# A Toeplitz chunk's eight lag matrices stored side by side, loaded as 4 KB rows and read by TensorE with a step of eight

## What is computed

```python
ew = jnp.exp(wc); ek = jnp.exp(k)             # k = v = the context
Af, Bf = _wkv_scan(ek, v, ew)                 # forward: A_t = sum_{i<t} e^{(t-1-i)w + k_i} v_i, B_t without v
Ab, Bb = _wkv_scan(ek[:, ::-1], v[:, ::-1], ew)
cur = jnp.exp(uc + k)
wkv = (Af + Ab + cur * v) / (Bf + Bb + cur)
return jax.nn.sigmoid(r) * wkv                # r = layernorm(x)
```

## Time and profile before

| | before |
|---|---|
| median of 3 runs | 212.69 us (212.09 to 212.9) |
| the profiled execution's own time | 211.43 us |
| its span | 209.7 us |
| mean granted TensorE clock | 0.949 |
| busy in the span: PE, DVE, ACT, POOL | 172.9, 166.8, 157.4, 138.7 us |
| 26 loads of lag matrices | 512 KB each, median 7.3 us from issue to landing |

### The profile page before, as it was taken

One profiled execution on the slowest core, in us unless ns is written; L12 is line 12 of the kernel. 1 busy time (PEld: TensorE's weight loads), 2 busy tenths in 40 slices (PEclk: granted clock), 3 DMA queues, 4 the chain that ended last, 5 costly groups with the idle time before them and its releaser, 6 DMA issues.

```text
span 209.7 us, 3447 instructions
## 1 busy us (share of the span) xinstructions
PE 172.9 (82%) x1146; PEld 125.8 (60%) x1146; DVE 166.8 (80%) x352; ACT 157.4 (75%) x242; POOL 138.7 (66%) x163
## 2 busy tenths in 40 slices
PE   4489996989899989988137987969889997789990
PEld 4456536989899989978126662324334432467780
DVE  0769586365755949999969968999799999889994
ACT  3459698737698699599879996958978891899910
POOL 3355223638869979986788852848897664058983
PEclk9969997899999999999855899999999999999998
DMA  3999999999999998500000000000000000025555
GB/s 89 331 375 348 349 328 292 296 283 297 278 292 319 243 250 216 159 28 2 0 0 0 0 3 2 0 0 0 0 3 0 0 0 2 3 76 171 171 185 200
DMA packets 43328, 29.31 MB, mean 140 GB/s; under 512 B 2224, under 2 KB 43056, under 8 KB 43312
## 3 DMA queue, kind: packets, MB, share of 16 engines
q1 hardware_dynamic: 42896, 28.58, 47.7%
q10 hardware_dynamic: 416, 0.52, 0.7%
HBM read 24.65 MB, written 4.46 MB: 139 GB/s over the span
## 4 chain that ended last, share of the span: by engine, by line
PE 34%; DVE 27%; ACT 17%; DMA 10%; issue 7%; POOL 3%; SPq 1%; DVEq 0%; ACTq 0%
PE ps L1019 10%; PE ps L1123 9%; DMA hidden<-lag_w 6%; PE ps L1159 5%; PE ps L1003 5%; DVE hidden L893 4%; DMA hidden<-in_ctx 4%; ACT hidden L551 3%; ACT z_t L702 2%; DVE hidden L911 2%; PE ps L1050 2%; DVE h_peaks L922 2%; ACT hidden L627 2%; ACT silu_out L681 2%; DVE z_t L964 2%
## 5 line engine op out<-in xcount | busy, mean ns | idle before, releaser
L1019 PE MATMUL ps<-hidden 128*128 128x128 f32 (+1 forms) x512 | 60.4, 280 | 6.0 <-DVE hidden L723 2.5
L1019 PEld LDWEIGHTS ps<-hidden 128*128 128x128 f32 x512 | 59.5, 196 | 7.4 <-issue 3.3
L922 DVE TENSOR_REDUCE h_peaks<-hidden (+2 forms) x24 | 26.0, 1122 | 2.0 <-POOL hidden L476 1.3
L418 POOL TENSOR_TENSOR x_all<-x_all,silu_out 128x512 f32<-128x512 f32 x15 | 22.9, 1542 | 6.3 <-DVE silu_out L792 6.3
L780 DVE SCALAR_TENSOR_TENSOR h_space<-z_t,ps 128x256 f32<-128x256 f32 x32 | 19.1, 598 | 8.6 <-PE ps L1019 8.2
L1159 PE MATMUL ps<-wdT,z_t 128*128 128x256 bf16 x192 | 22.6, 272 | 2.5 <-DVE z_t L964 2.3
L681 ACT ACTIVATE silu_out<-ps,mix_scale 128x1024 f32<-128x1024 f32 (+1 forms) x18 | 18.4, 1020 | 5.8 <-PE ps L1123 3.4
L1159 PEld LDWEIGHTS ps<-wdT,z_t 128*128 128x128 bf16 x192 | 17.6, 97 | 7.7 <-DVE z_t L964 2.9
L1043 PE MATMUL ps<-ident,hidden 128*128 128x128 f32 x64 | 11.6, 342 | 10.0 <-POOL hidden L457 8.5
L792 DVE SCALAR_TENSOR_TENSOR silu_out<-ps,small,silu_out 128x256 f32<-128x256 f32 x32 | 15.1, 476 | 5.5 <-ACT silu_out L532 3.4
L521 ACT ACTIVATE z_t<-x_all,mr,nr 128x256 f32<-128x256 f32 x32 | 16.4, 588 | 3.6 <-POOL mr L380 3.6
(11 more groups left out here) (116 smaller groups left out, 374.0 us busy)
## 6 DMA issues: line engine op xcount, KB each, us to landing
hidden<-lag_w SPq DMA_DIRECT2D x26, 512.0 KB, 7.3
x_all<-in_x SPq DMA_DIRECT2D x8, 512.0 KB, 8.9
hidden<-in_ctx SPq DMA_DIRECT2D x8, 512.0 KB, 9.1
out<-x_all SPq DMA_DIRECT2D x15, 256.0 KB, 2.1
xq<-in_L_ffn_w_down SPq DMA_DIRECT2D x1, 704.0 KB, 6.1
xq<-in_L_ffn_w_gate SPq DMA_DIRECT2D x1, 640.0 KB, 6.9
h_space<-in_L_ffn_w_up SPq DMA_DIRECT2D x1, 640.0 KB, 6.2
out<-x_all ACTq DMA_DIRECT2D x1, 256.0 KB, 2.4
```

What stands on the lines that cost most here:

```text
L418: nc.gpsimd.tensor_tensor(xs, xs, mixed[:, m % 2, :, :].rearrange("p c b -> p b c"), ALU.add).then_inc(s["x1_done"], 1)
L922: nc.vector.tensor_reduce(h_peaks[:, bass.ds(KA * b + k, 1)], hidden[:, bass.ds(b * HB + k * BT, cols)], AX.X, ALU.max, apply_absolute_val ...
L1019: last = nc.tensor.matmul(ps[:, j % BANKS, c * 2 * SEQS:end * 2 * SEQS], lag_tile(j)[:, c, :], ekp[:, (j * CK + c) * 2 * SEQS:(j * CK + en ...
```

## The change

`lag_dram` becomes [32 chunks, 4 quarters, 64 distances x 8 channels]: for each distance the eight values of a chunk's channels stand side by side. What partition p of a matrix needs is then one run of 128 x 8 values (4 KB) that starts 8 values later than that of partition p - 1, so a load has 128 rows of 4 KB instead of 1024 rows of 512 bytes; the bytes are the same. In the slot the eight matrices are interleaved, and PE reads the weights of one channel with a step of eight elements (32 bytes). The row of values is made on 128 partitions (quarter q of chunk j on partition 32q + j): POOL writes four pieces of distances, DVE multiplies distance by w, ACT takes one exponential over 512 columns, and ACT stores four quarters. For that, w is loaded four times and u once in small pieces ahead of x on SP's queue. `MADE` has three chunks instead of six, so 29 chunks are loaded instead of 26; the three that are made keep the old layout. The turn of the last feed-forward weights moves behind chunk 31, and the two small steps on the clip factors move from m = 12 and 13 to m = 9 and 10.

```diff
-    MADE = 10, 14, 18, 22, 26, 30
+    SET = CK
+    QUARTERS = 4
+    QL = 2 * T // QUARTERS
+    MADE = 10, 14, 18
...
         def lag_tile(j):
-            return ring[(GROUPS + j) % SLOTS].rearrange("p (g t) -> p g t", t=T)
+            tile = ring[(GROUPS + j) % SLOTS]
+            if j in MADE:
+                return tile.rearrange("p (c t) -> p c t", t=T)
+            return tile.rearrange("p (g t i) -> p g i t", t=T, i=SET)
+
+        def lag_matrix(j, c):
+            return lag_tile(j)[:, c, :] if j in MADE else lag_tile(j)[:, c // SET, c % SET, :]
...
-                src = bass.AP(lag_dram, j * CK * LAGS, [[1, P], [LAGS, CK], [1, T]])
-                sp.dma_start(lag_tile(j), src).then_inc(ring_in[(GROUPS + j) % SLOTS], 16)
+                src = bass.AP(lag_dram, j * CK * 2 * T, [[SET, P], [1, SET * T]])
+                sp.dma_start(ring[(GROUPS + j) % SLOTS], src).then_inc(ring_in[(GROUPS + j) % SLOTS], 16)
...
-                sp.dma_start(wu[:, 0:CG], w.rearrange("a b (p i) -> p (a b i)", i=CG)).then_inc(s["w_in"], 16)
-                sp.dma_start(wu[:, CG:2 * CG], u.rearrange("a b (p i) -> p (a b i)", i=CG)).then_inc(s["u_in"], 16)
+                for q in range(QUARTERS):
+                    sp.dma_start(w_rows[q * CHUNKS:(q + 1) * CHUNKS, :], w.rearrange("a b (j c) -> j (a b c)", c=CK)) \
+                        .then_inc(s["w_in"], 16)
+                sp.dma_start(u_rows[OWN_ROWS, :], u.rearrange("a b (j c) -> j (a b c)", c=CK)).then_inc(s["u_in"], 16)
...
-            nc.gpsimd.iota(lag_row[:, 0:T], [[-1, T]], base=T - 2, channel_multiplier=0,
-                           allow_small_or_imprecise_dtypes=True).then_inc(s["lags_set"], 1)
-            nc.gpsimd.iota(lag_row[:, T:LAGS], [[1, T - 1]], base=0, channel_multiplier=0,
-                           allow_small_or_imprecise_dtypes=True).then_inc(s["lags_set"], 1)
+            for q in range(QUARTERS):
+                nc.gpsimd.iota(lag_row[q * CHUNKS:(q + 1) * CHUNKS, :], [[(-1, -1, 1, 1)[q], QL]],
+                               base=(T - 2, QL - 2, 0, QL)[q], channel_multiplier=0,
+                               allow_small_or_imprecise_dtypes=True).then_inc(s["lags_set"], 1)
...
-                for i in range(CG):
-                    nc.scalar.activation(lag_w[:, i, :], lag_row, ACT.Exp, scale=wu[:, i:i + 1]) \
-                        .then_inc(s["lag_done"], 1)
+                act.wait_ge(s["lag_product"], 1)
+                nc.scalar.activation(lag_flat, lag_flat, ACT.Exp).then_inc(s["lag_done"], 1)
...
-                act.dma_start(lag_dram[:, :], lag_w.rearrange("p i j -> p (i j)")).then_inc(s["lag_stored"], 16)
+                for q in range(QUARTERS):
+                    act.dma_start(lag_dram[:, q, :], lag_flat[q * CHUNKS:(q + 1) * CHUNKS, :]).then_inc(s["lag_stored"], 16)
...
-                if m == 12:
+                if m == 9:
                     exp_clips()
...
+            nc.vector.tensor_tensor(lag_w, lag_row.rearrange("p (l o) -> p l o", o=1).broadcast_to([P, QL, CK]),
+                                    w_rows.rearrange("p (o c) -> p o c", o=1).broadcast_to([P, QL, CK]), ALU.mult) \
+                .then_inc(s["lag_product"], 1)
...
-                    last = nc.tensor.matmul(ps[:, j % BANKS, c * 2 * SEQS:end * 2 * SEQS], lag_tile(j)[:, c, :],
+                    last = nc.tensor.matmul(ps[:, j % BANKS, c * 2 * SEQS:end * 2 * SEQS], lag_matrix(j, c),
...
-                if j in (14, 23, 30):
-                    turn_weights((14, 23, 30).index(j))
+                if j in (14, 23):
+                    turn_weights((14, 23).index(j))
+            turn_weights(2)
```

More of the change, by code:

```diff
@@ L69, in gated_rwkv_ffn @@
     OWN_SEQS = 8
+    assert QUARTERS * CHUNKS == P and QL == T // 2
     assert T == P and IR == P // 2 and UNIT == 512 and CH == 2 and 2 * HALF == 512 and CG == 2
@@ L129, in gated_rwkv_ffn @@
         lnd = up_out[:, 0:512]
-        lag_w = up_out[:, 512:512 + CG * LAGS].rearrange("p (i j) -> p i j", i=CG)
+        lag_flat = up_out[:, 512:512 + QL * CK]
+        lag_w = lag_flat.rearrange("p (l c) -> p l c", c=CK)
         flat_row = down_row[:, :, :].rearrange("p j c -> p (j c)")
@@ L136, in gated_rwkv_ffn @@
         own_parts = [up_out[:, 512:1024], own[:, :]]
-        lag_row = down_row[:, :, :].rearrange("p j c -> p (j c)")[:, 0:LAGS]
+        lag_row = flat_row[:, 0:QL]
         xq_flat = xq[:, :, :, :, :].rearrange("p a b c d -> p (a b c d)").bitcast(F32)
@@ L158, in gated_rwkv_ffn @@
         up_even = [up_out[:, :], h8_space[:, BT:2 * BT]]
-        lag_dram = nc.dram_tensor("lag_w", [P, CG * LAGS], F32, kind="Internal")
+        lag_dram = nc.dram_tensor("lag_w", [CHUNKS, QUARTERS, QL * CK], F32, kind="Internal")
         ps = stack.enter_context(nc.psum_tensor("ps", [P, 8, 512], F32))
@@ L211, in gated_rwkv_ffn @@
         S = {n: small[:, i:i + 1] for i, n in enumerate(names)}
-        wu = small[:, 16:16 + 2 * CG]
+        w_rows = small[:, 32:32 + CK]
+        u_rows = small[:, 40:40 + CK]
+        OWN_ROWS = slice(CHUNKS, 2 * CHUNKS)
         down_scale = small[:, 24:26]
@@ L235, in gated_rwkv_ffn @@
             "gate_in", "up_in", "down_in", "g_x_in", "g_f_in", "clx_in", "cld_in", "w_in", "u_in",
-            "ones_set", "ident_set", "flip_set", "lags_set", "lag_done", "lag_stored", "lag_abs_set", "lag_abs_done", "w_all_in", "u_all_in", "u_all_done", "own_done", "made_exp", "made",
+            "ones_set", "ident_set", "flip_set", "lags_set", "lag_product", "lag_done", "lag_stored", "lag_abs_set", "lag_abs_done", "w_all_in", "u_all_in", "u_all_done", "own_done", "made_exp", "made",
             "tanh_done", "clips_done", "prep",
@@ L311, in load_weights @@
                     sp.dma_start(down[:, :, I:KA * P], src[:, :, KI * P:I]).then_inc(weights_in[m], 16)
-            with nc.allow_non_contiguous_dma("256 values, once"):
-                sp.dma_start(wu[:, 0:CG], w.rearrange("a b (p i) -> p (a b i)", i=CG)).then_inc(s["w_in"], 16)
-                sp.dma_start(wu[:, CG:2 * CG], u.rearrange("a b (p i) -> p (a b i)", i=CG)).then_inc(s["u_in"], 16)
+            with nc.allow_non_contiguous_dma("256 values, five times"):
+                for q in range(QUARTERS):
+                    sp.dma_start(w_rows[q * CHUNKS:(q + 1) * CHUNKS, :], w.rearrange("a b (j c) -> j (a b c)", c=CK)) \
+                        .then_inc(s["w_in"], 16)
+                sp.dma_start(u_rows[OWN_ROWS, :], u.rearrange("a b (j c) -> j (a b c)", c=CK)).then_inc(s["u_in"], 16)
             load_values("g_x", g_xattn)
@@ L330, in _ @@
             sp.dma_start(u_all, u.rearrange("a b c -> (a b) c").broadcast_to([P, C])).then_inc(s["u_all_in"], 16)
-            sp.wait_ge(s["lag_stored"], 16)
+            sp.wait_ge(s["lag_stored"], 16 * QUARTERS)
             for j in range(CHUNKS):
@@ L352, in _ @@
         def _(pool):
-            nc.gpsimd.iota(lag_row[:, 0:T], [[-1, T]], base=T - 2, channel_multiplier=0,
-                           allow_small_or_imprecise_dtypes=True).then_inc(s["lags_set"], 1)
-            nc.gpsimd.iota(lag_row[:, T:LAGS], [[1, T - 1]], base=0, channel_multiplier=0,
-                           allow_small_or_imprecise_dtypes=True).then_inc(s["lags_set"], 1)
+            for q in range(QUARTERS):
+                nc.gpsimd.iota(lag_row[q * CHUNKS:(q + 1) * CHUNKS, :], [[(-1, -1, 1, 1)[q], QL]],
+                               base=(T - 2, QL - 2, 0, QL)[q], channel_multiplier=0,
+                               allow_small_or_imprecise_dtypes=True).then_inc(s["lags_set"], 1)
+            pool.wait_ge(s["lags_set"], QUARTERS)
             nc.gpsimd.memset(ones[:, :], 1.0).then_inc(s["ones_set"], 1)
@@ L434, in _ @@
             pool.wait_ge(s["pad_set"], 2)
-            pool.wait_ge(s["lag_stored"], 16)
+            pool.wait_ge(s["lag_stored"], 16 * QUARTERS)
             nc.gpsimd.iota(lag_abs, [[1, T]], base=1 - T, channel_multiplier=1,
@@ L498, in lag_weights @@
             def lag_weights():
-                act.wait_ge(s["lags_set"], 2)
-                act.wait_ge(s["w_in"], 16)
-                for i in range(CG):
-                    nc.scalar.activation(lag_w[:, i, :], lag_row, ACT.Exp, scale=wu[:, i:i + 1]) \
-                        .then_inc(s["lag_done"], 1)
-                act.wait_ge(s["u_in"], 16)
-                act.wait_ge(s["lag_done"], CG)
-                nc.scalar.activation(lag_w[:, :, T - 1], wu[:, CG:2 * CG], ACT.Exp).then_inc(s["lag_done"], 1)
-                act.wait_ge(s["lag_done"], CG + 1)
-                act.dma_start(lag_dram[:, :], lag_w.rearrange("p i j -> p (i j)")).then_inc(s["lag_stored"], 16)
+                act.wait_ge(s["lag_product"], 1)
+                nc.scalar.activation(lag_flat, lag_flat, ACT.Exp).then_inc(s["lag_done"], 1)
+                act.wait_ge(s["u_in"], 16)
+                act.wait_ge(s["lag_done"], 1)
+                nc.scalar.activation(lag_w[OWN_ROWS, QL - 1, :], u_rows[OWN_ROWS, :], ACT.Exp).then_inc(s["lag_done"], 1)
```

(12 more changed lines are left out.)

## The result

The changed kernel takes 266.55 us (median of 4 runs, 265.27 to 266.83) against 212.66 for the kernel before: a ratio of 1.253, 95% interval 1.249 to 1.257. That is 53.9 us slower, outside the stated range and further out than the prices given for the first rival.

The account below looks back on a forecast made before the run. It took PE, paced by weight loads, as the limit up to about 79 us, then PE and DVE both. -4.8 us at the last denominator plus 1.26 at the start gave -3.5, so 212.69 to 209.2 us; range 206.8 to 213.8.

Parts of the forecast that it names:

- Reading with a step of eight: PE's 464 weight loads in the chunks: surcharge between 0 and 67 ns each, taken as 0.
- rival 1: PE's 464 weight loads get slower by up to 67 ns each, giving 238 to 240 us; chance 0.2.
- the weight load sets PE's pace: PE in the chunks: about 112 ns for 128 columns, and nothing hides a slower load.
- Rival 2: Chunk loads stay at 290 GB/s and PE's DMA waits remain, giving about 212.4 us; chance 0.12.
- rival 3: Residuals still block DVE's small instructions at the stage's end: only 1.2 us faster, 211.5 us; chance 0.1.
- The rest of the sum: Whole kernel without a read surcharge: -4.8 at the last denominator plus 1.26 at the start, -3.5 us.
- Start: Three more small issues ahead of x on SP's queue make x and the context 1.26 us later.
- Waits for DMA and made matrices: PE's waits in the chunks go: 0.85 and 0.89 us for DMA, 0.75 and 1.09 for made matrices.
- DVE's block: DVE at the stage's end: scales begin 2.5 us earlier, small instructions beside an idle POOL save 2.3 us.
- From the first chunk to the last denominator: The last denominator starts 4.8 us earlier before the start's delay, the later of PE's 4.9 and DVE's 4.8.

Follow-up runs that it names:

- e1: The changed kernel with PE reading 128 neighbouring values as a channel's weights instead of every eighth; 208.37 us, ratio 0.984.
- e3: One execution of the kernel before with chunks read in different steps; per weight load 112 ns in order, 119 at step 2, 238 at step 8.
- e8: The changed kernel with four channels side by side instead of eight (2 KB rows, 16-byte step); 263.54 us in one execution.
- e4: The changed kernel with two channels side by side instead of eight (1 KB rows, 8-byte step); 211.65 us, ratio 0.997.
- e9: e7 with 26 idle products at the start instead of 12; 209.34 us, ratio 0.988.
- e2: The kernel before, old layout, with only three made chunks, last weights' turn behind chunk 31 and clip steps at m = 9 and 10; 209.57 us, ratio 0.988.
- e7: e5 with chunks 8, 10 and 14 made instead of 10, 14 and 18; 208.88 us, ratio 0.985.
- e5: e2 with the small loads of w and u on ACT's queue instead of SP's; 209.56 us, ratio 0.987.
- e10: e6 with 26 idle products at the start instead of 12; 209.43 us, ratio 0.988.
- e6: e4 with the five small loads of w and u on ACT's queue instead of SP's; 209.35 us, ratio 0.989.

## Why the prediction was wrong

**The step that failed** is *Reading with a step of eight*: "I take 0". It measured 126 ns per weight load. By that pace it is 464 x 126 ns = 58.5 us, and between the chunk stages of the changed kernel and e1 there are 58.0 (117.3 and 59.3). Two errors stand in it. The value was taken from the row of ACT, but L513 reads PSUM with a far step, and the weights lie in SBUF; e3 shows that PE's reads of SBUF cost by the 16-byte line. The rows that do read SBUF with far steps (L780, L418 in the earlier trace rows) both showed a surcharge, and they were set aside for a reason that no row bore out. And the upper bound was too low: it carried over a surcharge per value from other engines. PE pays 1.86 ns per value in all, against 0.87 in order, so 0.99 more where DVE pays 0.48 and POOL 0.52 more. Taken as a ratio, the same rows would have given less still: 598 for 476 and 1542 for 1274 are factors of 1.26 and 1.21, where PE's is 2.1. No row of the trace before bounds PE's price; one chunk read with a step, as in e3, measures it.

The Trainium skill, "Advanced Engine Details and Errata", SBUF Cachelines, spoke against the change: 16-byte lines, at least two hits on each. The runs agree with it and give its figure: one value per line costs 2.1 times the load in order, two per line 6% more than it. It spoke for a higher chance of rival 1 than 0.2.

**What held.** That the weight load sets PE's pace, so that nothing hides a slower one: right, 58.0 of the 58.5 us arrive in the span. Rival 1 had the place and the sign; its price of 28 to 31 us was half. Rival 2 (loads no faster) is refuted: 389 GB/s, where two rows gave 415. So is rival 3 (DVE's chain stays): its two instructions take 0.59 us together in e1, for 2.67.

**The rest of the sum** was -3.5, and e1 measured -4.1 by the medians. That these are close is in part luck. The sum was made for the span, and e1's traced execution, the fastest of its five, has a span 5.6 us shorter than before (204.1 for 209.7). By terms of that trace:

- Start, +1.26: the issue of the first context load moved by 1.38 (3.77 to 5.15 us). The chunks begin 1.49 later in e1, 1.65 in e8, 2.83 in the changed kernel and 2.83 in e4. The part over 1.4 is not the same from run to run. With it go the time of the first context load (7.20, 7.36, 8.13 and 7.84 us from issue to landing) and the granted clock from 15 to 20 us (0.89, 0.90, 0.74 and 0.71). No run separates the two, and e9 does not let me call the clock the cause.
- Waits for DMA and made matrices: gone, as predicted.
- DVE's block: 276 ns for 1315, and 0.17 us for 0.83, as predicted. In e1 PE alone sets the last denominator, so this term is not to be seen in the time by itself.
- From the first chunk to the last denominator, -4.8 predicted, measured 59.3 us (35.01 to 94.31) for 66.3, so -7.0. The term was under-sized because 96 matmuls took 12.53 us at the beginning of the chunks before, 131 ns each, when PE ran at a granted clock of 0.71 from 35 to 40 us; in e1 the clock there was 1.00. The sum had left that in. It accounts for 1.6 of the 2.2 us that the term was short.
- Layout and small edits: by the medians e2 gets 2.9 of e1's 4.1 us with 512-byte rows. By the traces it is the other way round: from the start of the span to the last denominator e1 is 3.1 us ahead of e2 (94.31 for 97.43), since PE's 3.9 us of waits for DMA are gone, and e2 is 2.4 ahead of before, of which 1.4 to 1.6 are the clock.

So the change was three things: a layout worth 1.2 us by the medians and 3.1 by the traces, small edits worth 2.9 by the medians and about 1 by the traces without the clock, and a read that costs 58. How the small gain divides stays open. A version that beats both kernels is e7, 208.88 us at 0.985 of before, with the old layout.

## What to carry to other kernels

A layout that makes a transfer's rows longer by interleaving moves the cost to whoever reads them: count the 16-byte lines that PE touches, for weights and for the moving operand alike, and keep two float32 values on each. Before trading, see which unit paces the stage; a unit without cover pays each added nanosecond times its number of instructions, here 464. And try the small edits of a change by themselves: here they gave 2.9 us by the medians and needed nothing of the large one. For differences of 1 us, look in the trace at where they arise. Here a dip of the granted clock in a part that nobody changed was worth as much.

## What the runs showed of the hardware

- PE's reads of SBUF in float32 cost about 1.8 ns per 16-byte line, with a floor of 112 ns per 128 values, on the weight side and on the moving side: 119 ns at step 2, 174 at step 3, 222 to 238 from step 4 to 8. Pairs of neighbours with jumps of 64 bytes and fours with jumps of 128 bytes cost nothing on the moving side (112 ns).
- Overlapping rows of lag values came at 389 GB/s with 4 KB (after, 35 to 40 us), 380 with 2 KB (e8), 350 with 1 KB (e4) and 290 with 512 bytes (before). The fixed cost per row that two sizes gave (9.8 ns) gets the 4 KB rate to within 7%.
- Two DVE TENSOR_SCALAR of 128x128 float32 took 276 ns each with POOL idle, and 1315 ns each beside POOL's L418 and L411.
- An earlier issue is not an equally earlier landing. For the first context load, 0.95 us earlier became 0.30 in e5, and 1.38 us later became 1.20 in e1 and 2.13 in the changed kernel.
- Some 40 us behind the last denominator the granted clock fell in every trace from e3 to e10 (to 0.66 from 135 to 140 us in e5 and e6) and in none of before, after, e1 and e2; the part behind the chunks then took 111.5 to 111.8 us instead of 109.8 to 110.4. What brings it is open.
